# A gated MLP with adapters: its first stretch rebuilt, with four adapter groups in buffers of their own and row operands in blocks

## What is computed

```python
x = x + conv(x) * mask                 # a long convolution per channel
x = x + einsum('bsi,boi->bso', x, w1[ids1])   # a 1024x1024 matrix picked per sequence
x = x + einsum('bij,bkj->bik', x, w2[ids2])   # once more, other ids
# gated MLP, F = 2752, with a rank-16 adapter picked per sequence (ids3), scale 0.5
gate = x @ Wg.T + 0.5 * (x @ Ag[id].T) @ Bg[id].T
up   = x @ Wu.T + 0.5 * (x @ Au[id].T) @ Bu[id].T
act  = silu(gate) * up
x = x + act @ Wd.T + 0.5 * (act @ Ad[id].T) @ Bd[id].T
```

## Time and profile before

| | us |
|---|---|
| median of 3 runs (2184.78 to 2189.65) | 2187.39 |
| the profiled execution, its own time | 2185.16 |
| its span, first to last instruction | 2183.5 |
| PE busy in the span | 2087.3 |
| last transpose of layer three | 665.48 |
| first matmul of the MLP | 672.17 |
| S1 by T1 of the first unit starts | 738.23 |
| last matmul starts | 2175.32 |

### The profile page before, as it was taken

One profiled execution on the slowest core, in us unless ns is written; L12 is line 12 of the kernel. 1 busy time (PEld: TensorE's weight loads), 2 busy tenths in 40 slices (PEclk: granted clock), 3 DMA queues, 4 the chain that ended last, 5 costly groups with the idle time before them and its releaser, 6 DMA issues.

```text
span 2183.5 us, 34214 instructions
## 1 busy us (share of the span) xinstructions
PE 2087.3 (96%) x10432; PEld 1774.5 (81%) x10432; DVE 1610.3 (74%) x2144; ACT 971.2 (44%) x1282; POOL 99.0 (5%) x167
## 2 busy tenths in 40 slices
PE   2998999999996899999999999999999999999998
PEld 2997888888885788888888888888888888878887
DVE  7777999999997778787877337458787878753433
ACT  2222888788883533333433325343333333333232
POOL 3110000000001230000000000000000000000000
PEclk9999999999998999999999999999999999999999
DMA  5999999989986664333434995444343434264543
GB/s 194 376 364 347 351 349 356 356 331 349 351 345 235 188 199 129 93 110 89 110 92 147 252 259 187 173 120 118 91 110 94 108 96 108 70 217 159 183 154 125
DMA packets 254658, 441.49 MB, mean 202 GB/s; under 512 B 146902, under 2 KB 147094, under 8 KB 234390
## 3 DMA queue, kind: packets, MB, share of 16 engines
q1 hardware_dynamic: 241046, 408.69, 56.4%
q0 software_dynamic: 11392, 32.01, 4.4%
q10 hardware_dynamic: 2176, 0.26, 0.1%
HBM read 400.74 MB, written 63.73 MB: 213 GB/s over the span
## 4 chain that ended last, share of the span: by engine, by line
PE 82%; DVE 8%; DMA 4%; ACT 2%; issue 2%; DVEq 1%; POOL 0%; ACTq 0%; SPq 0%; POOLq 0%
PE ps L1849 19%; PE ps L1850 19%; PE ps L1851 19%; PE ps L1793 4%; PE ps L1795 4%; PE ps L1794 4%; PE ps L1769 4%; DMA W<-in_w 3%; PE ps L1894 2%; PE ps L1893 2%; DVE wl L1318 2%; PE ps L1802 1%; PE ps L1925 1%; PE ps L1926 1%; DMA araw<-picked_a 1%
## 5 line engine op out<-in xcount | busy, mean ns | idle before, releaser
L1849 PE MATMUL ps<-bh,oph 128*128 128x512 f32 x1216 | 476.3, 392 | 9.2 <-ACT tmp L807 6.0
L1850 PE MATMUL ps<-bl,oph 128*128 128x512 f32 x1216 | 475.8, 391 | 0.0
L1851 PE MATMUL ps<-bh,opl 128*128 128x512 f32 x1216 | 474.2, 390 | 0.0
L1318 DVE TENSOR_TENSOR wl<-W,wh 128x2048 fp32r<-128x2048 f32 x152 | 343.6, 2285 | 9.9 <-ACT wh L742 9.0
L1406 DVE TENSOR_TENSOR tmp<-ps,tmp 128x512 f32<-128x512 f32 (+1 forms) x340 | 234.1, 689 | 132.0 <-PE ps L1894 67.5
L742 ACT ACTIVATE wh<-W 128x2048 fp32r<-128x2048 f32 x152 | 290.7, 1915 | 61.0 <-DMA W<-in_w 55.1
L1403 DVE TENSOR_TENSOR wdl<-wraw,wdh 128x1024 fp32r<-128x1024 f32 x92 | 112.6, 1224 | 264.2 <-ACT wdh L807 264.2
L1849 PE MATMUL ps<-acb_h,wdh 128*128 128x512 f32 (+1 forms) x736 | 280.8, 382 | 4.8 <-DVE acb_l L1403 4.8
L1850 PE MATMUL ps<-acb_l,wdh 128*128 128x512 f32 (+1 forms) x736 | 279.8, 380 | 0.0
L1851 PE MATMUL ps<-acb_h,wdl 128*128 128x512 f32 (+1 forms) x736 | 279.7, 380 | 0.0
L1849 PEld LDWEIGHTS ps<-bh,oph 128*128 128x128 f32 x1216 | 229.4, 189 | 54.6 <-DVE opl L1403 10.4
(11 more groups left out here) (205 smaller groups left out, 2794.9 us busy)
## 6 DMA issues: line engine op xcount, KB each, us to landing
W<-in_w SPq DMA_DIRECT2D x152, 1024.0 KB, 6.9
raw<-in_wgu SPq DMA_DIRECT2D x168, 256.0 KB, 2.7
wraw<-in_wd SPq DMA_DIRECT2D x84, 512.0 KB
toep<-kpad SPq DMA_DIRECT2D x32, 1024.0 KB, 9.3
lraw<-picked_b SPq DMA_DIRECT2D x88, 256.0 KB, 3.8
raw<-kept_acts SPq DMA_DIRECT2D x88, 256.0 KB, 3.4
kept_acts<-tmp SPq DMA_DIRECT2D x84, 256.0 KB, 2.3
picked_b<-in_lora_b POOLq DMA_DIRECT2D x32, 352.0 KB, 4.9
```

Of the source, the lines that this page charges most:

```text
L1318: V.tensor_tensor(out=wl[:, c], in0=W[:, c], in1=wh[:, c].bitcast(F32), op=ALU.subtract).then_inc(w_lo, 1)
L1849: mm(to, lhsT=wh, rhs=mh, start=start, stop=False)
L1850: mm(to, lhsT=wh, rhs=ml, start=False, stop=False)
L1851: return mm(to, lhsT=wl, rhs=mh, start=False, stop=stop)
```

## The change

- **Adapter groups.** All four of the first stage have a raw buffer (`graw`) and places for their parts (`gcut`, `aph`, `apl`, `last_low`). SP loads groups 0 and 1 behind the last chunk of `W`, without waiting for the splits; groups 2 and 3, `wlast`, `lt`'s source and two quarters of weights come after the third split of the last step. ACT copies groups 0, 1 and 2 before and between the two `copy_product`, DVE splits 0 and 1 before `add_last_half`.
- **Row operands.** `bh` and `bl` become 14 places (`rows`), with an order of their own (`HI`, `LO`). B11 and B21 are copied and split in four blocks of 128x512 each, and PE multiplies groups 0 and 1 with a block as soon as it is split.
- **Half unit.** `K0` and `K1` are cut into `kop`, beyond the places of `X`, and so needn't wait for the store of `X`. `K0` by B11 for the second tile moves ahead of groups 2 and 3.
- **Raw differences.** T3 and T4 are subtracted on POOL in the first stage. The splits of T2, T3 and T4 go into `half_unit`, their copies into ACT's (T2 ahead of the ranks).
- **Ranks.** `tmh` and `tml` move to 16384 bytes, groups of one tile share a PSUM bank, and mask, copies and splits of the ranks are made for two groups at once (half as many instructions, each twice as long).
- **Stores of X.** The first stage's half goes first; the mask doesn't wait for a store.
- **Panels.** The load of the first `resid` goes behind the loads of panel 4. In the last tile the last two panels go through output blocks 0 to 3 first, then 4 to 7, and SP stores the last tile in four pieces of 512 KB, as DVE adds them.

```diff
-RANK_BANK = (1, 2, 4, 0)
+RANK_BANK = (1, 2)
...
+            rows = [sb(s, f"rows{k}", [P, KH, TILE], F32R) for k in range(14)]
+        with placed(ROWS_AT + 10 * KH * TILE * 4, "graw") as s:
+            graw = sb(s, "graw", [P, GR, 2 * GS, LT, R])
+            gcut = sb(s, "gcut", [P, GR, LT, P], F32R)
...
@@ SP @@
+            def first_loads():
+                sp.wait_ge(lora_out, GATHERED)
+                group(0)
+                group(1)
+                sp.wait_ge(w_lo, before * WC + 3)
+                load_last()
+                group(2)
+                group(3)
+                load_ranks(0, 0)
+                for k in range(2):
+                    load_quarter(k, 1)
+                sp.wait_ge(rows_done, 1)
+                for k in range(2):
+                    part = slice(k * SEQ, (k + 1) * SEQ)
+                    sp.dma_start(xs[:, part], X[:, part]).then_inc(x_saved[k], 16)
+                next_last(0)
+                sp.wait_ge(cleared, 2)
+                load_down_ranks(0, 0)
...
@@ POOL @@
-            pool.wait_ge(x_saved[1], 16)
...
+            pool.wait_ge(mask_set, 4)
+            pool.wait_ge(ap_done, 4)
+            pool.tensor_tensor(out=by_rows(LO[T3]), in0=second_half(1), in1=X[:, TB:2 * TB, 0:KH],
+                               op=ALU.subtract).then_inc(t3_raw, 1)
+            pool.wait_ge(t3_raw, 1)
+            pool.wait_ge(t_raw, 2)
+            pool.wait_ge(ap_lo, 2 * GR)
+            pool.tensor_tensor(out=by_rows(LO[T4]), in0=second_half(0), in1=by_rows(LO[T2]),
+                               op=ALU.subtract).then_inc(t4_raw, 1)
             pool.wait_ge(x_saved[0], 16)
...
@@ ACT @@
+            group_hi_of(0)
+            act.wait_ge(w_lo, last_step * WC + (WC + 1))
+            group_hi_of(1)
+            copy_product(last_step, 0)
+            act.wait_ge(w_lo, last_step * WC + (WC + 3))
+            group_hi_of(2)
+            copy_product(last_step, 1)
+            act.wait_ge(half_added, 2)
+            blocks_hi_of(B11, 0, 0)
             act.wait_ge(rows_done, 1)
+            blocks_hi_of(B21, 0, 1)
             half_unit_hi(0)
             rows_hi_of(B22, 1, 1)
+            act.wait_ge(ap_done, 4)
+            group_hi_of(3)
+            raw_ready(1)
+            operand_hi(T1, rraw[HI[T2]][:])
             raw_ready(2)
+            operand_hi(T2, rraw[LO[T2]][:])
...
@@ ACT, half_unit: behind the two sigmoids; behind S3, A22, S4 @@
+                    operand_hi(T3, rraw[LO[T3]][:])
+                    operand_hi(T4, rraw[LO[T4]][:])
...
@@ DVE @@
+            group_lo_of(0)
+            group_lo_of(1)
+            add_last_half(last, 0, base - 1)
+            block_lo_of(B11, 0, 0, 0, 1)
+            add_last_half(last, 1, base - 1)
+            V.memset(tick[:, 6:7], 0.0).then_inc(rows_done, 1)
+            for k in range(1, KH):
+                block_lo_of(B11, 0, 0, k, k + 1)
+            for k in range(KH):
+                block_lo_of(B21, 0, 1, k, KH + k + 1)
             half_unit_lo(0)
+            group_lo_of(2)
+            sub(by_rows(rraw[HI[T2]][:]), rows_in(1, 0), rows_in(0, 0)).then_inc(t_raw, 1)
+            rows_lo_of(B22, 1, 1, 9)
+            group_lo_of(3)
+            operand_lo(T1, rraw[HI[T2]][:], 10)
             dve.wait_ge(t_raw, 1)
+            sub(by_rows(rraw[LO[T2]][:]), rows_in(1, 1), by_rows(rraw[HI[T2]][:])).then_inc(t_raw, 1)
             for st in range(NST):
-                for g in range(GR):
-                    ranks_part(st, g)
-                for g in range(GR):
-                    ranks_cut(st, g)
+                ranks_part(st, 0)
+                ranks_part(st, 1)
+                ranks_cut(st, 0)
+                ranks_lo(st, 0)
+                ranks_cut(st, 1)
                 half_unit(st)
...
@@ DVE, half_unit: behind the first four splits; behind the products of s1; behind the last three splits @@
+                    operand_lo(T2, rraw[LO[T2]][:], 11)
+                    operand_lo(T3, rraw[LO[T3]][:], 12)
+                    operand_lo(T4, rraw[LO[T4]][:], 13)
...
@@ PE @@
+            def first_rows():
+                pe.wait_ge(ap_lo, 4)
+                for k in range(KH):
+                    pe.wait_ge(bop_lo, k + 1)
+                    last = both(0, 0, B11, k, start=k == 0)
+                last.then_inc(ap_done, 1)
+                for k in range(KH):
+                    pe.wait_ge(bop_lo, KH + k + 1)
+                    last = both(0, 1, B21, k, stop=k == KH - 1)
+                last.then_inc(ap_done, 3)
+                pe.wait_ge(op_lo, cut_count(0, 0, 2))
+                row_blocks(bank(BANK_F), kop[:, 0], kop[:, 1], B11, start=True)
+                row_blocks(bank(BANK_D), kop[:, 0], kop[:, 1], B11, start=True)
+                pe.wait_ge(op_lo, cut_count(0, 0, 6))
+                row_blocks(bank(BANK_F), kop[:, 2], kop[:, 3], B21)
+                pe.wait_ge(ap_lo, 8)
+                for k in range(KH):
+                    both(2, 0, B11, k, start=k == 0)
+                pe.wait_ge(bop_lo, 2 * KH + 2)
+                for k in range(KH):
+                    both(2, 0, T1, k)
+                for k in range(KH):
+                    last = both(2, 1, B22, k, stop=k == KH - 1)
+                last.then_inc(ap_done, 4)
+                row_blocks(bank(BANK_D), kop[:, 0], kop[:, 1], T1)
+                row_blocks(bank(BANK_D), kop[:, 2], kop[:, 3], B22)
```

More of the change, by code:

```diff
@@ L297, in build @@
         cleared = sem("cleared")
+        group_in = [sem(f"group_in{g}") for g in range(GR)]
         araw_in = sem("araw_in")
@@ L447, in load_rest @@
                     load_projection(st, g)
-                for half in range(2):
-                    sp.wait_ge(op_lo, cut_count(st, 0, 2 + 4 * half))
-                    load_quarter(2 + half, 1)
+                next_last(st)
                 sp.wait_ge(ap_lo, st * 2 * GR + 2 * GR)
@@ L1395, in _ @@
                     cut_chunk(base, 3)
-                else:
-                    add_last_half(last, 1, base - 1)
-            dve.wait_ge(step_added, base + 2)
-            V.memset(tick[:, 6:7], 0.0).then_inc(rows_done, 1)
             def sub(to, a, b):
@@ L1858, in blocks, with rank_block @@
                                  start and k == 0, stop and k == KH - 1)
                 return last
-            def project(st, g, half, operands, start, stop):
+            def blocks(to, slot, i, start=False, stop=False):
+                return row_blocks(to, oph[:, slot], opl[:, slot], i, start, stop)
+            def rank_block(g, hi, lo, half, i, k, start=False, stop=False):
+                cols = slice(g % 2 * GC, (g % 2 + 1) * GC)
+                at = half * KH + k
+                return three(ps[:, RANK_BANK[g // 2], cols], hi[:, at], lo[:, at], rows[HI[i]][:, k, cols],
+                             rows[LO[i]][:, k, cols], start and g % 2 == 0, stop and g % 2 == 1)
@@ L1863, in project @@
+            def project(st, g, half, operands):
                 pe.wait_ge(ap_lo, st * 2 * GR + 2 * g + half + 1)
-                to, cols = ps[:, RANK_BANK[g], 0:GC], slice(g % 2 * GC, (g % 2 + 1) * GC)
-                for i in operands:
+                for n, i in enumerate(operands):
                     for k in range(KH):
-                        last = three(to, aph[:, half * KH + k], apl[:, half * KH + k], bh[:, i, k, cols], bl[:, i, k, cols],
-                                     start and i == operands[0] and k == 0, stop and i == operands[-1] and k == KH - 1)
+                        last = rank_block(g, aph, apl, half, i, k, half == 0 and n == 0 and k == 0,
+                                          half == 1 and k == KH - 1)
@@ new lines, in first_tile_ranks, with both @@
+                project(st, g, 1, (B21,))
+            def second_tile_ranks(st, g):
+                project(st, g, 0, (T1, B11))
+                project(st, g, 1, (B22,))
+            def first_rows():
+                def both(first, half, i, k, start=False, stop=False):
+                    for g in (first, first + 1):
+                        last = rank_block(g, group_hi[g], group_lo[g], half, i, k, start, stop)
+                    return last
+                pe.wait_ge(ap_lo, 4)
[18 more added lines that the diff above has]
+                    both(2, 0, T1, k)
+                for k in range(KH):
+                    last = both(2, 1, B22, k, stop=k == KH - 1)
+                last.then_inc(ap_done, 4)
+                row_blocks(bank(BANK_D), kop[:, 0], kop[:, 1], T1)
+                row_blocks(bank(BANK_D), kop[:, 2], kop[:, 3], B22)
@@ L1962, in unit @@
                 pe.wait_ge(op_lo, cut_count(st, u, A22))
+                if first and st == 0:
+                    pe.wait_ge(bop_lo, 13)
                 if not first:
```

387 lines of the change are left out of this document (205 added, 182 removed).

## The result

The changed kernel takes 2177.99 us (median of 6 runs, 2175.71 to 2181.79), the kernel before 2186.61 in runs beside it: ratio 0.9957, 95% interval 0.9944 to 0.9971. That is 9.4 us less by the ratio. It is faster, but by a little under half of the 19.9 us forecast, and 2178 lies outside the range of 2160 to 2176. The profiled execution took 2176.47 us, its span is 2174.8, 8.7 less than the earlier trace rows.

A forecast was written before the change was run, and what follows sets the result against it. PE was taken as the bound (82% of the last-ending chain), so only its standstills could pay. Gains 16.4 (beginning) + 1.7 (second stage) + 1.8 (end) = 19.9 us, from 2187.39 to 2167.5, range 2160 to 2176.

The forecast's parts named there:

- the last panel's own wait: Last panel: operands ready 3.2 us after the panel before starts, PE wants them after 2.7; 0.5 us lost.
- Steps 1 to 9: First stage's beginning, from rows_done to S1 by T1 in the first unit: 738.23 becomes 721.8, gain 16.4 us.
- Step 4: Beginning: POOL's raw T3 difference takes 4.0 us (bounds 2.3 to 5.3), during which DVE's two-input subtractions stand still.
- step 6: Beginning: ACT copies T2 and ranks, POOL subtracts T4, DVE masks and splits; PE gets its ranks at 699.1 without a wait.
- The rival in which they run side by side: Beginning: POOL and DVE don't block each other, the 4.0 us vanish; 2163.5 us, 14 in 100.
- the rival of a slow POOL: Beginning: POOL takes 8 us, costing 4 more at T3 and 4 more before lt; gain 12, 2175.4 us, 7 in 100.
- The second stage: Second stage's beginning: ranks in pairs bring copy_p1 1.7 us earlier; gain 1.7 (0 to 2.5).
- The end: Last panels and stores: smaller last store saves 2.3, a last-panel wait loses 0.5; gain 1.8 us (0.5 to 3).
- The first part of the clock's: First 48 matmuls, between block splits, at half rate, PE 4.6 us later; whole clock rival 2171.5 us, 17 in 100.
- The second part: 24 matmuls after PE's stall ahead of groups 2 and 3 at half rate, 2.9 us later; whole clock rival 17 in 100.
- ACT did not wait for groups 0 to 2: Slower-than-before rival: late loads of groups 0 and 1 hold ACT ahead of the product copy at 661.65; 2192, 3 in 100.
- the units have no waits: No-change rival: beginning's gain lost in the units, DVE 4 us behind and PE waiting in each; 2187 us, 4 in 100.
- the forecast's own case: Whole kernel: gains of beginning, second stage and end sum to 19.9 us; 2167.5 us, 2164 to 2171, 55 in 100.

The follow-up runs named there:

- experiment 5: Changed kernel with POOL's T3 difference also waiting for T2's raw difference, so it starts about 10 us later; ratio 0.9935 to the kernel before.
- experiment 7: Changed kernel with the copies of P1 out of PSUM right behind ScalarE's first copy of the second matrix; ratio 0.9969 to the kernel before.
- the last one: Changed kernel with residual in pieces, both beginnings reordered on ACT and DVE, and bank-freeing sums first in each unit; 2160.74 us, ratio 0.9898 to the kernel before.
- experiment 4: Changed kernel with both raw differences, T3 and T4, back on DVE right behind T2's, ahead of the mask; ratio 0.9942 to the kernel before.
- experiment 1: Kernel before with only each stage's first resid load (2 MB) moved behind the loads of panel 4; ratio 1.0028 to the kernel before.
- experiment 8: Changed kernel with the old end: last panels in one loop, last rows of y stored by POOL in 1 MB; ratio 0.9967 to the kernel before.
- experiment 6: Changed kernel with raw differences T3 and T4 on VectorE behind the first rank mask; ratio 0.9956 to the kernel before.
- experiment 9: Changed kernel with both beginnings reordered on ACT and DVE, residual loads left as in the changed kernel; ratio 0.9944 to the kernel before.

## Why the forecast was wrong

**The step that failed** is the move of the first `resid` load, costed at "nothing either way, at worst 1 us". It costs some 10 us in the profiled pair's panels (of the 10.4, 0.4 is the last panel's own wait, which was forecast) and 5 to 6 in time, shown from both sides: 6.1 slower when it is put into the kernel before, 5.7 and 5.2 faster when it is taken out of the changed one. I reckoned that panel 5's loads "have one panel of 5.4 us to spare", and left out four things. A 2 MB load ahead of them takes longer than that by itself (8.1 us from issue to landing in the trace of before). The buffer of panel 5 is the one that a later panel needs, so its delay is handed on. And the second 2 MB stand ahead of that later panel: two late loads in series, where I looked at one. And PE restarts at a lower granted clock after the wait (0.66), which adds 1.4 us to each. It happens twice, once a stage.

**Steps 1 to 9, the beginning, held in their sum.** S1 by T1 came 15.4 us earlier in relation to the last transpose (719.99 - 662.62 = 57.37 against 72.75 before), where 16.4 was forecast. In detail, less the 2.86 by which this execution is earlier: the products by kept weights (`K0`) start 1.1 late (671.83 for 670.7), those by groups 2 early (680.01 for 682.0), since POOL did not hold DVE up; the ranks of PE are there at 696.49 for 696.2; `copy_p1` has its 5.79 for 6.

**Step 4 was wrong in its mechanism and right in its sum.** I let POOL's difference take 4.0 us and block DVE for them. Alone it takes 4.62 (experiment 5). The figure of the Trainium skill, "GPSIMD Engine Reference", Performance versus the Vector engine, 4497 ns for an addition of this size, agrees. But DVE was not blocked: POOL was, for 14.55 us. The time came back in step 6, where ACT's copies wait for T3 and T4 by their written order (2.62 and 2.09 us). So the rule of "SBUF — State Buffer", Who interferes with whom, in the Trainium skill, that the two exclude each other, bears on this case in one direction only: between back-to-back subtractions of DVE, POOL got almost no turn, and DVE lost nothing until its row had a gap. The rival in which they run side by side had DVE's half of it right and missed who pays; the rival of a slow POOL had a length of 8 us where 14.55 came, but put its price on DVE.

**The second stage**, 1.7 forecast, gave nothing. The wait for `copy_p1` is 2.60, as the 2.53 of the earlier trace rows. The copy of `lt` now stands between the two groups of rank copies on ACT and waited 1.72 us there for its own load, which the forecast didn't look at. In experiment 7 and the last one this stretch is 2.8 and 3.3 us shorter than in the changed kernel, 1.0 and 1.5 shorter than in the kernel before, so the stage does have something to give. On top, the profiled pair has 1.6 us that don't seem to be an effect of the change: the twelve matmuls behind that wait took 2.82 us before and 4.37 after (1460.46 to 1464.83, the first one 0.76 long). Of the nine profiled executions that stop there for 2.5 to 2.6 us, those of before and of experiment 4 stayed at full rate and seven went slow, that of experiment 1 among them, which has the old code in this place.

**The end** gave 2.7 less 0.44 of wait in the last panel, so 2.3 for 1.8 forecast; the 2.7 are confirmed by the trace of experiment 8.

**The rivals.** None of them was the case as a whole. The first part of the clock's did happen: beside the block splits PE was granted 0.80 of its clock from 663.9 to 665.9 us and 0.50 to 667.9, and the first `K0` product started at 671.83, 0.7 behind its split. The second part didn't: PE did not stop ahead of groups 2 and 3, and their matmuls ran at full rate, 0.120 us each. (That part was also priced too high: 4.6 us for 48 matmuls is 0.095 each, and by that 24 are 2.3, not 2.9.) ACT did not wait for groups 0 to 2, and the units have no waits. With the residual in pieces the forecast's own case comes back in part: 14.6 us by the ratio, 16.0 in span (14.2 without the layers ahead). By its marks the rest to 19.9 is mainly the second stage's units (3.4 us), the first panels (1.3) and the beginning (1.0).

## What to carry to other kernels

A large transfer has no slack of its own: when it is moved past a queue of small ones, follow each load behind it to its landing, and from there to the next load that waits for the same buffer; each may be late by little, and the two together by more than the slack. Here it helped to load it early, or in pieces with one behind each small load and the second one elsewhere. And ask of the longest wait in a row of waits what ends next behind it: `copy_p1` had 5.8 us and alone was worth nothing in the first stage; with DVE's order behind it changed too, the profiled stretch got 7.0 us shorter (2.8 in time, unresolved).

## What the runs showed of the hardware

GpSimd and VectorE did not share evenly. A 128x2048 two-input subtraction on POOL took 4.62 us with DVE idle or little used and 14.55 us beside a row of DVE's. It ended 4.6 us after the start of the last instruction of that row (682.13 to 686.70), just what it takes alone, so it had hardly moved in the ten us before; and DVE's subtractions of the same size kept the 2.28 us that they take without POOL. When DVE's were short and alone, it paid as well: a pair of 64x512 splits that takes 1.38 took 3.19 beside POOL's second subtraction.

Whether PE restarts at full or at half rate after a stop of 2.5 to 2.6 us differed from one profiled execution to the next in the same place, also between kernels that have the same code there: the twelve matmuls behind the stop took 2.8 us in two of nine and 4.0 to 4.4 in seven, and the twenty up to S1 by T1 took 1.4 to 1.6 more. What decides between the two stays open, and one profiled pair can show a difference of that size that no edit made.

What stays open is why the edits to the beginning, 3.6 us in the stretch of units in experiment 6 and 7.0 in experiment 9, show as 0 and 2.8 us in the timed runs, while with the residual in pieces they show 7.4 (0.9933 to 0.9899). The intervals of these differences, some 4 us, hold most of it. The scatter of the first panels (240 to 253 us) is as large as these; it goes with PE's short waits, and what makes those come and go was not looked for.
